# Moving the rest of the setup of an attention kernel into its first turns, and filling a tensor in 32 pieces from another queue

## What is computed

```python
xn = layernorm(x, g_in)                       # x: 16 x 512 rows of 512
q  = (xn @ Wq).reshape(b, n, 16, 64) * 64 ** -0.5
k, v = split(xn @ Wkv)                        # one head of 64, plus one null key and value
sim = einsum('bhid,bjd->bhij', q, [null_k, k]) + [null_bias, attn_bias]
sim = where(causal, neg, sim); sim = where([True, mask], sim, neg)
out = softmax(sim) @ [null_v, v]
y   = layernorm(out @ Wo, g_out)
# then: rms norm, router logits, top-k tokens of each expert,
# gelu(xe @ fc1 + b1) @ fc2 + b2, gated, scattered back, added to x
```

## Time and profile before

| | us |
|---|---|
| median of 3 runs (2059.53 to 2068.98) | 2060.33 |
| the profiled execution | 2061.54 |
| its span, first to last instruction | 2059.8 |

### The profile page before, as it was taken

The page is one execution under the profiler, slowest core; times in us unless marked ns, Lnnn a source line. Parts: engine busy times, 40 slices in busy tenths (PEclk is TensorE's granted clock), DMA queues, the critical chain, the costliest instruction groups (busy, mean ns, idle before and its releaser), DMA issues.

```text
span 2059.8 us, 41248 instructions
## 1 busy us (share of the span) xinstructions
PE 1868.0 (91%) x12276; PEld 1655.9 (80%) x12276; DVE 1549.8 (75%) x2411; ACT 1318.7 (64%) x2624; POOL 1204.8 (58%) x1173
## 2 busy tenths in 40 slices
PE   1788999997238999999999999999999999999996
PEld 1667888886138899899989898888998888988895
DVE  5778888885786777787777778777787877777763
ACT  3656767663535667676676766667676666766663
POOL 1566777774225566574755657566574756656551
PEclk9899999998559999999999999999999999999998
DMA  5766444432933344342534435253443435434351
GB/s 191 235 191 182 113 113 113 113 103 58 316 101 104 103 139 111 125 138 97 148 92 138 116 114 148 89 141 99 141 127 110 131 103 139 111 127 126 104 129 31
DMA packets 96107, 263.08 MB, mean 128 GB/s; under 512 B 20433, under 2 KB 22193, under 8 KB 93105
## 3 DMA queue, kind: packets, MB, share of 16 engines
q1 hardware_dynamic: 79026, 228.21, 35.0%
q0 software_dynamic: 17024, 34.19, 8.8%
HBM read 223.47 MB, written 55.60 MB: 135 GB/s over the span
## 4 chain that ended last, share of the span: by engine, by line
PE 65%; DVE 4%; ACT 2%; issue 1%; POOL 1%; DMA 0%; DVEq 0%; ACTq 0%; POOLq 0%
PE experts_b_a L2172 17%; PE experts_b_y L272 11%; PE experts_b_y L273 11%; PE experts_b_y L274 11%; PE experts_b_b L2172 9%; PE experts_b_c L2172 4%; ACT experts_h L1684 2%; PE experts_b_turn L2152 1%; DVE experts_x_lo L1838 1%; PE experts_b_turn L2161 1%; PE experts_b_c L2161 1%; POOL experts_rows L1508 0%; DVE experts_w_lo L1898 0%; PE experts_b_a L2258 0%; POOL experts_rows_meta L1495 0%
## 5 line engine op out<-in xcount | busy, mean ns | idle before, releaser
L272 PE MATMUL experts_b_y<-experts_w_hi,experts_h_hi 128*128 128x512 f32 x1024 | 406.8, 397 | 0.0
L273 PE MATMUL experts_b_y<-experts_w_lo,experts_h_hi 128*128 128x512 f32 x1024 | 404.7, 395 | 0.0
L274 PE MATMUL experts_b_y<-experts_w_hi,experts_h_lo 128*128 128x512 f32 x1024 | 399.6, 390 | 0.0
L1470 POOL TENSOR_TENSOR experts_s_raw<-experts_w_raw 128x256 f32<-128x256 f32 x128 | 136.4, 1065 | 423.3 <-DMA experts_w_raw<-in_w 422.7
L2172 PE MATMUL experts_b_a<-experts_x_hi,experts_w_hi 128*128 (+1 forms) x1024 | 290.5, 284 | 9.5 <-ACT experts_u_copy L1652 4.1
L2172 PE MATMUL experts_b_a<-experts_x_hi,experts_w_lo 128*128 (+1 forms) x1024 | 290.3, 284 | 0.0
L2172 PE MATMUL experts_b_a<-experts_x_lo,experts_w_hi 128*128 (+1 forms) x1024 | 290.1, 283 | 0.0
L274 PEld LDWEIGHTS experts_b_y<-experts_w_hi,experts_h_lo 128*128 128x128 f32 x1024 | 192.7, 188 | 43.4
L2172 PEld LDWEIGHTS experts_b_a<-experts_x_hi,experts_w_hi 128*128 128x128 f32 x1024 | 195.2, 191 | 29.7 <-issue 7.5
L272 PEld LDWEIGHTS experts_b_y<-experts_w_hi,experts_h_hi 128*128 128x128 f32 x1024 | 194.4, 190 | 24.0
L273 PEld LDWEIGHTS experts_b_y<-experts_w_lo,experts_h_hi 128*128 128x128 f32 x1024 | 194.6, 190 | 21.3
(11 more groups left out here) (366 smaller groups left out, 5585.5 us busy)
## 6 DMA issues: line engine op xcount, KB each, us to landing
experts_w_raw<-in_w SPq DMA_DIRECT2D x256, 512.0 KB
attend_bias<-in_bias SPq DMA_DIRECT2D x68, 256.0 KB, 3.9
attend_spread_w<-weight_dram SPq DMA_DIRECT2D x34, 512.0 KB, 6.6
xn_dram<-g_out_row SPq DMA_DIRECT2D x6, 2304.0 KB, 9.7
attend_q_x<-in_x SPq DMA_DIRECT2D x17, 256.0 KB, 3.0
attend_k_x<-in_x SPq DMA_DIRECT2D x17, 256.0 KB, 6.0
xn_dram<-attend_xn SPq DMA_DIRECT2D x17, 256.0 KB, 4.0
experts_b_sb<-in_b SPq DMA_DIRECT2D x16, 256.0 KB
```

Source lines behind the costliest of these rows:

```text
L272: nc.tensor.matmul(out, lh, rh, start=first, stop=False)
L273: nc.tensor.matmul(out, lh, rl, start=False, stop=False)
L274: return nc.tensor.matmul(out, ll, rh, start=False, stop=last)
L1470: nc.gpsimd.tensor_tensor(s1, a21, a22, ALU.add).then_inc(s_done, 1)
```

## The change

Five things are changed.

- **The list.** DVE names only the first half of the places (a = 0) in the setup, by the new function `name_pairs`. The second half (`other_places`) is done in `attend` ahead of DVE's first turn. The list's way through DRAM (`share_list`) moves into SP's turn 0, and SP reads the query and key tile of pair 0 straight from `kl_i`. All engines wait for the row (`kl_in`) after turn 0.
- **The weights.** In the setup ACT rounds wkv and half of wq; the other half of `wq_hi` is written ahead of ACT's first turn (`split_wq`), and the `lo` parts are written in DVE's turn 0 (`split_first`). TensorE waits for them (`lo_done`). The raw weights now lie in tiles of the attention that turn 0 and 1 don't use (`bias`, `sc`, the rows of y and xn), and the columns of the list in `spread_w`.
- **The loads.** `load_query(0)` and `load_key(0)` come first in SP's turn 0, and `load_wo(j)` stands behind `load_key(j)` instead of at the head of turn j.
- **The start values** are set by POOL, `logits` too.
- **The fill** is issued by ACT in 32 pieces of 256 rows (512 KB), from `in_g_out` in DRAM: four in the setup and four in each of the first seven turns (at its head, behind `query_norm`, behind `key_norm`, and at its end). `store` waits for all 32.

```diff
+PIECES, FIRST_PIECES = 32, 4
...
-                sp.dma_start(wkv_raw[:, :, :], io["wkv"]).then_inc(raw_in[0], 16)
-                sp.dma_start(wq_raw[:, :, :], io["wq"]).then_inc(raw_in[1], 16)
+                sp.dma_start(keep["wkv_raw"], io["wkv"]).then_inc(raw_in[0], 16)
+                for a in range(2):
+                    sp.dma_start(keep["wq_raw"][a], io["wq"][:, a * KD // 2:(a + 1) * KD // 2, :]).then_inc(raw_in[1], 16)
...
-                sp.wait_ge(lists_done, 1)
-                sp.dma_start(keep["kl_dram"].rearrange("(a p) c -> p a c", p=P), kl_i[:, :, :]).then_inc(lists_out, 16)
-                sp.wait_ge(lists_out, 16)
-                sp.dma_start(keep["kl"][:, :], keep["kl_dram"].rearrange("(o p) c -> o (p c)", o=1)).then_inc(lists_in, 16)
-                sp.wait_ge(lists_in, 16)
...
+                for piece in range(FIRST_PIECES):
+                    fill(nc.scalar, io, keep, piece)
                 act.wait_ge(gain_in, 16)
...
+                act.wait_ge(raw_in[0], 16)
+                for k in range(KD):
+                    nc.scalar.activation(keep["wkv_hi"][:, k, :], keep["wkv_raw"][:, k, :], ACT.Copy, scale=g_col[:, k:k + 1])\
+                        .then_inc(keep["hi_done"], 1)
+                act.wait_ge(raw_in[1], 32)
+                for k in range(KD // 2):
+                    nc.scalar.activation(keep["wq_hi"][:, k, :], keep["wq_raw"][0][:, k, :], ACT.Copy, scale=g_col[:, k:k + 1])\
+                        .then_inc(keep["hi_done"], 1)
                 act.wait_ge(hidden_done, 1)
+                act.wait_ge(keep["hi_done"], KD + KD // 2)
...
+                step.step(nc.vector.tensor_scalar(diag, diag, 0.0, None, ALU.is_equal))
+
+                name_pairs(nc, step, keep, 0, slot[:, 0:1], hit_k[:, :])
+                step.step(nc.vector.tensor_scalar(keep["kl_f"][:, 0, 7:8], rank_k[:, NT * QT - 1:NT * QT], 1.0 - DEPTH, 1.0,
                                                   ALU.add, ALU.max))
...
-                for n, (raw, hi, lo) in enumerate(splits):
-                    dve.wait_ge(hi_done, n + 1)
-                    for k in range(KD):
-                        step.inc(nc.vector.scalar_tensor_tensor(lo[:, k, :], raw[:, k, :], g_col[:, k:k + 1],
-                                                                f32(hi[:, k, :]), ALU.mult, ALU.subtract))
-                dve.wait_ge(const_in, 6 * 16)
-                step.inc(nc.vector.tensor_scalar(keep["null_bias"][:, :], keep["null_bias"][:, :], -1.0, None, ALU.mult))
+                step.step(nc.vector.tensor_copy(keep["kl_i"][:, 0, :], keep["kl_f"][:, 0, :]))
+                step.inc(nc.vector.tensor_copy(keep["hit"][:, 0:1], slot[:, 1:2]))
                 step.inc(nc.vector.memset(keep["hidden"][:, NT, :], MASKED))
-                step.inc(nc.vector.memset(keep["logits"][:, :, :], 0.0))
                 step.wait()
+                keep["steps"] = step.n
+
+
+def name_pairs(nc, step, keep, a, slot, hit_k):
+
+    kl, hit = keep["kl_f"], keep["hit"]
+    step.step(nc.vector.scalar_tensor_tensor(hit_k, keep["rank_k"], slot, keep["pairs"], ALU.is_equal, ALU.mult))
+    for c, column in ((0, "key_tile"), (2, "bias_tile"), (3, "off_diag"), (4, "query_tile"), (6, "carry")):
+        step.step(nc.vector.scalar_tensor_tensor(keep["junk"], hit_k, 1.0, keep[column], ALU.mult, ALU.mult,
+                                                 accum_out=kl[:, a, c:c + 1]))
...
+def fill(engine, io, keep, piece):
+
+    rows = N // PIECES
+    engine.dma_start(keep["xn_dram"][piece * rows:(piece + 1) * rows, :], io["g_out"].to_broadcast([rows, D]))\
+        .then_inc(keep["xn_filled"], 16)
...
+            if eng is nc.sync and isinstance(row, int) and row == 0 and column in (0, 4):
+                return eng.value_load(keep["kl_i"][0:1, 0, column:column + 1], min_val=least, max_val=most)
...
+                if j == 0:
+                    eng.wait_ge(kl_in, 17)
...
-                    sp.wait_ge(keep["xn_filled"], 16 * DEPTH)
-                    sp.dma_start(keep["xn_dram"][bass.ds(at * P, P), :], xn[:, :]).then_inc(xn_out, 16)
-
-                def fill(j):
-                    tiles = slice(j * NT // DEPTH, (j + 1) * NT // DEPTH)
-                    sp.dma_start(keep["xn_dram"][0:N, :].rearrange("(t p) d -> p t d", p=P)[:, tiles, :],
-                                 keep["g_out"][:, :].unsqueeze(1).to_broadcast([P, tiles.stop - tiles.start, D]))\
-                        .then_inc(keep["xn_filled"], 16)
-
-                sp.dma_start(null_col[:, :], io["null_v"]).then_inc(null_in, 16)
+                    sp.wait_ge(keep["xn_filled"], 16 * PIECES)
...
+                def share_list():
+                    sp.wait_ge(keep["lists_done"], 1)
+                    sp.dma_start(keep["kl_dram"].rearrange("(a p) c -> p a c", p=P), keep["kl_i"][:, :, :]).then_inc(lists_out, 16)
+                    sp.wait_ge(lists_out, 17)
+                    sp.dma_start(keep["kl"][:, :], keep["kl_dram"].rearrange("(o p) c -> o (p c)", o=1)).then_inc(kl_in, 16)
 
                 def turn(j, on, upto, edge):
-                    if edge and on(0) and j < 2:
-                        load_wo(j)
+                    if edge and on(0) and j == 2:
+                        sp.wait_ge(keep["lo_done"], 2 * KD)
...
+                    if edge and on(0) and j == 0:
+                        sp.dma_start(null_col[:, :], io["null_v"]).then_inc(null_in, 16)
+                        share_list()
+                    if edge and on(0) and j < 2:
+                        load_wo(j)
...
-                    if edge and on(0):
-                        fill(j)
...
+                pool.memset(state[:, 1, :, :], 0.0).then_inc(begun, 1)
...
+                pool.wait_ge(null_in, 17)
+                nc.gpsimd.tensor_copy(flat(state[:, 0, :, :]), null_col[:, :].to_broadcast([P, KO * P])).then_inc(begun, 1)
...
+                def split_wq(k):
+                    nc.scalar.activation(keep["wq_hi"][:, k, :], keep["wq_raw"][1][:, k - KD // 2, :], ACT.Copy,
+                                         scale=keep["g_col"][:, k:k + 1]).then_inc(keep["hi_done"], 1)
+
+                def fill_piece(j, n):
+                    fill(nc.scalar, io, keep, FIRST_PIECES + 4 * j + n)
+
+                for k in range(KD // 2, KD):
+                    split_wq(k)
...
+                    if edge and on(0):
+                        fill_piece(j, 0)
...
                         query_norm(j)
+                        if edge:
+                            fill_piece(j, 1)
...
                         key_norm(j)
+                        if edge:
+                            fill_piece(j, 2)
...
+                    if edge and on(0):
+                        fill_piece(j, 3)
...
-                nc.vector.memset(state[:, 1, :, :], 0.0).then_inc(begun, 1)
...
-                dve.wait_ge(null_in, 17)
-                nc.vector.tensor_copy(flat(state[:, 0, :, :]), null_col[:, :].to_broadcast([P, KO * P])).then_inc(begun, 1)
-                dve.wait_ge(begun, 1 + CONSTANTS)
+                def other_places():
+                    step = Count(dve, keep["setup_step"], keep["steps"])
+                    hit_k = sc_list
+                    name_pairs(nc, step, keep, 1, keep["hit"][:, 0:1], hit_k)
+                    nc.vector.tensor_copy(keep["kl_i"][:, 1, :], keep["kl_f"][:, 1, :]).then_inc(keep["lists_done"], 1)
+
+                def split_first(name, k):
+                    raw = keep["wkv_raw"][:, k, :] if name == "wkv" else keep["wq_raw"][k // (KD // 2)][:, k % (KD // 2), :]
+                    dve.wait_ge(keep["hi_done"], (0 if name == "wkv" else KD) + k + 1)
+                    nc.vector.scalar_tensor_tensor(keep[name + "_lo"][:, k, :], raw, keep["g_col"][:, k:k + 1],
+                                                   f32(keep[name + "_hi"][:, k, :]), ALU.mult, ALU.subtract)\
+                        .then_inc(keep["lo_done"], 1)
+
+                sc_list = flat(q_null[:, :, :])[:, 0:NT * QT]
+                other_places()
...
                         key_stats(j)
+                        if edge and j == 0:
+                            for k in range(KD):
+                                split_first("wq", k)
...
                         query_rows(j)
+                        if edge and j == 0:
+                            for k in range(KD):
+                                split_first("wkv", k)
+                            dve.wait_ge(keep["const_in"], 6 * 16)
+                            nc.vector.tensor_scalar(keep["null_bias"][:, :], keep["null_bias"][:, :], -1.0, None, ALU.mult)\
+                                .then_inc(keep["consts_ready"], 1)
+                            dve.wait_ge(keep["consts_ready"], 1)
...
                 def keys_values(n):
+                    if isinstance(n, int) and n == 0:
+                        pe.wait_ge(keep["lo_done"], 2 * KD)
...
                 def queries(n, a):
+                    if isinstance(n, int) and n == 0:
```

(1 more changed line is left out.)

131 lines of the change are left out of this document (59 added, 72 removed).

## The result

The changed kernel takes 2084.61 us (median of 6 runs, 2077.08 to 2086.55), the kernel before beside it 2059.93 (6 runs, 2055.99 to 2068.98). The ratio is 1.0109, with a 95% interval of 1.0084 to 1.0134: slower by 1.1%, where 2042 us had been forecast. The profiled execution took 2086.55 us with a span of 2084.8, 25.0 us more than before.

The account below looks back on a forecast made before the run. The setup's DVE chain and late loads were taken to bound the start, TensorE the full turns. Terms -14.3 - 8 + 1 (ACT's issues) + 3 = -18.3 us gave 2043.2, as a median 2042 us; range 2030 to 2053.

Parts of the forecast that it names:

- SP's first issue of q_x: Start of the attention: with the setup ending near 18.5 us, q_x of pair 0 is issued at 19.6, 10.2 us earlier.
- First query rows: Turn 0: DVE begins on q_x of pair 0 at 23.7 us, between bounds of 22.6 and 24.4.
- POOL's start values are hidden: Before the first product: POOL's memsets, some 4 us from 18.5 on, end before `q_mv` is there at 24.6 us.
- the moved `wq_lo` costs no more than this: Before the first product: DVE's branch with `wq_lo` ends 1.3 us after the old one, its whole cost.
- The two branches: From `q_st` to the first product: the old one through POOL, ACT and TensorE until 29.2 us, DVE's own until 30.5.
- The gain of 9.7: First product at 31.5 us instead of 41.12, with bounds of 8.9 to 10.7 us.
- -14.3 and -8: Turn 1 starts 14.3 us earlier (bounds 10 to 15.5); fills off SP's queue gain 8 us (bounds 0 to 17).
- 2.2 us each at the fill's rate: Fill in the early turns: loads meet 512 KB pieces of 2.2 us each beside them, not a whole fill ahead.
- slower: Rival, chance 0.04: DRAM-to-DRAM pieces above about 4.5 us each starve the loads; at 6 us each, 2075 us.
- the full turns: From 200 to 300 us: taken as bound by TensorE, busy for 96.55 of 100 us.
- the new wait of the first store: First `store` waits for all pieces: SP stands for 12 us, priced at 3 us once, with ends 0 and 12.

Follow-up runs that it names:

- e3: The changed kernel with its 32 pieces read from the row on chip, the first four issued at the end of ACT's setup: 2049.28 us, 0.9973.
- e9: The changed kernel with the fill back as seven transfers on SP's queue and three increments ahead of DVE's turns: 2048.76 us, 0.9952.
- e12: The changed kernel with its pieces copied from 256 different rows of x each instead of one row of g_out: 2053.02 us, 0.9981.
- e1: The changed kernel with the fill back as seven transfers on SP's queue from the row on chip: 2063.3 us, 1.0036.
- e5: The changed kernel with pieces read from the row on chip and three increments ahead of DVE's turns: 2031.63 us, 0.9845.

## Why the prediction was wrong

- **Right: SP's first issue of q_x.** Forecast 19.6 us, measured 18.96. The step behind it was wrong: I put the four pieces after `hidden` and at ACT's cost (1.7 us), which made ACT the last engine of the setup at 18.0 us. They were issued beside it, ACT was through at 16.10, and DVE was the last at 17.49. Its forecast was 17.4.
- **Failed: "First query rows", 23.7 us.** Measured 33.44. Its upper end was DVE's 4.83 us from issue to use, taken from a time in which little else was under way. The pieces were named as the reason to go near that end, yet they cost three times as much.
- **Failed: "POOL's start values are hidden".** I priced the memsets and not the transfer that the last of them waits for, which I listed as moved to SP's turn 0. It landed after 14.8 us, and POOL began on `q_r` at 37.83 us, 3.4 us after DVE had the mean (34.46); before it was 0.3 us. Also with the good source in e3 POOL copies at 27.44 us only.
- **Failed: "the moved `wq_lo` costs no more than this" (1.3 us).** The two branches were summed as if they ran side by side without touching. `wq_lo` stretched the other branch: `q_r` and `q_b` took 1.51 and 1.79 us beside it, against 0.55 and 0.26 in turn 1, so that the old branch was the later one. `wq_lo` ended at 42.25 us and DVE then waited 2.94 us for `qx_hi`. In e9, where q_x is early and the transfers are not slow, the first product comes at 32.94 us, and in e3 at 37.27, not at 31.5. (The gain of 9.7 is 9.6 by its own numbers.)
- **Right in sum by luck, off in its terms: -14.3 and -8.** With a source that doesn't starve the loads (e3) turn 1's transposes start at 45.43 us against 54.67: -9.2, below my lower bound of 10. From pair 4 to pair 7 a turn takes 22.2 us there, and not 24 to 25. Together pair 7 is 21.7 us early, forecast 22.3 (14.3 + 8), because the second term came out at 12.5. e9 and e3 split it in another way: 9.9 us from the moved setup, 11.8 from the fill in 32 pieces on ACT's queue. By the rule of the Trainium skill that I weighed ("DMA: Bandwidth & Descriptors", section "Issuing engines are not separate DMA queues") another queue alone would give 0. The 11.8 us don't decide this: e3 has both another queue and pieces of 512 instead of 2304 KB, and no run has small pieces on SP's queue or the seven fills on ACT's.
- **Failed: the rate of a piece, "2.2 us each at the fill's rate".** Measured 11.0 us in the changed kernel. This is the main error. The rival "slower" (0.04) was this mechanism, with its threshold at 4.5 us per piece. I gave it too little, though I had written that no row showed such a copy, and I had not noticed that all 8192 rows read the same 2 KB. How much of it is the one address and how much the form of the packets stays open (e12). It cost 26.4 us at pair 7, and together with the 2.6 us by which e12 falls short of the forecast it is the whole way from -22.3 to +6.7.
- **Failed, and in no rival: the full turns.** I wrote that TensorE bounds them, by its 96.55% of busy time, and took them as unchanged. TensorE is nearly full and still hangs on DVE's weights once per turn. The eight turns from pair 8 on cost 16.5 us more (8 times 2.07); turn 7 had given 2.4 back. Without the hold-up the changed kernel would be near 2068 us (an estimate, 2084.6 - 16.5), still not faster.
- **Right: the new wait of the first store.** Forecast 12 us of standing for SP; it stood from 180.4 to 192.72. The price of 3 us was too high: POOL waited 5.04 us for the bias parts behind it, but DVE only 0.36 and 0.57 us for POOL, and turn 7 took 23.0 us instead of 25.5.
- **Not tested:** from pair 16's q_x to the last store it takes 129.95 us instead of 121.96. Of these 8.0 us turn 16, also held up, is 2.2 (26.87 us from store to store instead of 24.66). e1 and e12 lose 7.9 and 5.9 us there, e3 and e5 nothing (121.6 and 121.5). The router adds nothing. The experts give 3.8 us back, within their spread.

6.7 (to pair 7) + 14.1 (to pair 16) + 8.0 (to the last store) - 3.8 (experts) = 25.0 us, the difference of the spans. The best version, e5, is the change with the pieces read from chip and three idle instructions: 0.9845 (0.9827 to 0.9863) and 0.9858 (0.9832 to 0.9885), so 1.4 to 1.6% faster than before.

## What to carry to other kernels

Price a moved transfer by its source's address pattern as well as by its bytes: a broadcast read from one row in DRAM is one to avoid, and a row that already stands on chip is better. When a step is moved, look at what its last instruction waits for, not only at its engines' time, and at what runs beside it at its new place: a DVE product with two on-chip inputs stretched POOL's small operations from 1.3 to 4.5 us. In a loop that repeats exactly, look for short DVE operations with two on-chip inputs that start near the end of a POOL operation: there 0.1 us decides over 2 us per turn, any edit elsewhere can shift it, and a delay on the engine that has time to spare can be the cure. Compare a loop's turn length in both traces before blaming the edit.

## What the runs showed of the hardware that I had not expected

- A copy of 512 KB whose 256 reads all hit one row of 2 KB in DRAM takes 11.0 us to land, with different rows (and larger packets) 4.7 us, from chip 4.0 us. What runs beside it suffers: 0.5 KB took 14.8 us, against 2.9 in e12.
- ACT's queue issued four transfers that wait for nothing at 5.62 us, while ACT's operation of 7.03 us, begun at 5.61, was still running.
- DVE's idle time around one register load is 0.78 or 0.89 us by the place of the same code: 0.89 at instruction 414 (seven kernels), 0.78 at 417, 430 and 478.
- With the load at its old place, `kept_sum` was free in every loop turn behind the first at 1.16 to 1.19 us behind POOL's start, held up in every one at 1.27 or more, and either at 1.20 to 1.23. The hold-up was 1.2 to 1.4 us, but in three turns of e12 it was 3.78 to 3.79, which stays open.
